# One scan and one readout over both halves of a piece, where its two PSUM banks are neighbours

## The reference

```python
    delta = jax.nn.softplus(jnp.einsum('blr,dr->bld', dt_low, dt_proj_w) + dt_proj_b)
    A = -jnp.exp(A_log)                                   # [512 channels, 16 states]
    dA = jnp.exp(delta[..., None] * A)                    # decay
    dBu = delta[..., None] * B_var[:, :, None, :] * ut[..., None]   # drive
    def step(h, inp):
        da, dbu, c = inp
        h = da * h + dbu                                  # the scan over 512 tokens
        y = jnp.einsum('bdn,bn->bd', h, c)                # the readout
        return (h, y)
    ...
    y = y + ut * D_param
    out_z = y * jax.nn.silu(z)
    return jnp.einsum('bld,ed->ble', out_z, out_proj_w)
```

## Time and profile before

| | us |
|---|---|
| median of 3 runs (lowest, highest) | 2031.44 (2030.55, 2032.27) |
| the profiled execution, its own time | 2028.13 |
| its span, first to last instruction | 2026.3 |
| DVE busy over the span | 1505.6 (74%) |
| PE busy over the span | 1654.3 (82%) |
| ACT, POOL busy over the span | 998.0 (49%), 893.1 (44%) |

### The profile page before, as it was taken

One profiled execution on the slowest core, in us unless ns is written; L12 is line 12 of the kernel. 1 busy time (PEld: TensorE's weight loads), 2 busy tenths in 40 slices (PEclk: granted clock), 3 DMA queues, 4 the chain that ended last, 5 costly groups with the idle time before them and its releaser, 6 DMA issues. The chain is left out here.

```text
span 2026.3 us, 22042 instructions
## 1 busy us (share of the span) xinstructions
PE 1654.3 (82%) x6616; PEld 740.2 (37%) x6616; DVE 1505.6 (74%) x2254; ACT 998.0 (49%) x1524; POOL 893.1 (44%) x662
## 2 busy tenths in 40 slices
PE   7398999999999999999977669596886959678466
PEld 7262534436252543526233124141332414133032
DVE  6436464564546465454658999999999999999998
ACT  3125335252534435252565756657475674747542
POOL 2610000000000000000249887969788796977863
PEclk9998989899898989999888778697887969778677
DMA  5573542526363351627234233424324332441420
GB/s 192 196 118 106 88 137 50 103 88 104 105 103 121 63 133 56 101 99 112 71 114 164 99 121 116 136 77 144 133 99 141 115 118 91 146 135 64 156 94 11
DMA packets 103331, 223.83 MB, mean 110 GB/s; under 512 B 12913, under 2 KB 65266, under 8 KB 99554
## 3 DMA queue, kind: packets, MB, share of 16 engines
q1 hardware_dynamic: 100194, 214.70, 38.4%
q0 software_dynamic: 3072, 8.37, 1.2%
HBM read 169.57 MB, written 53.48 MB: 110 GB/s over the span
## 5 line engine op out<-in xcount | busy, mean ns | idle before, releaser
L1322 POOL TENSOR_TENSOR work<-rep,bc 128x1024 f32<-128x1024 f32 x256 | 597.3, 2355 | 152.3 <-PE ps L1654 135.4
L1551 DVE TENSOR_TENSOR_SCAN ps<-ps,work 128x512 f32<-128x512 f32 x512 | 623.9, 1218 | 19.7 <-ACT ps L1444 11.4
L1444 ACT ACTIVATE ps<-rep,a_neg 128x512 f32<-128x512 f32 x512 | 343.7, 687 | 252.1 <-DVE work L1557 249.4
L830 DVE TENSOR_REDUCE m<-ps 128x1 f32<-128x512 f32 x512 | 327.8, 685 | 161.2 <-PE ps L965 158.3
L717 ACT ACTIVATE prob<-ps 128x1024 f32<-128x1024 f32 x256 | 257.7, 1021 | 235.8 <-PE ps L989 234.1
L1557 DVE TENSOR_TENSOR work<-ps,bc 128x512 f32<-128x512 f32 x512 | 344.1, 672 | 0.0
L1654 PE MATMUL ps<-work,pick 128*32 128x512 f32 x1024 | 181.4, 790 | 168.9 <-DVE work L1557 168.9
L635 POOL TENSOR_TENSOR m_parts<-m,nil 128x16 bf16<-128x16 f32 x32 | 7.1, 221 | 590.0 <-DVE m L830 590.0
L965 PE MATMUL ps<-k_st,q_st 96*128 96x512 bf16 x512 | 201.2, 438 | 31.7 <-DVE m L830 25.7
L1629 PE MATMUL ps<-xn_sb,front_w 128*128 128x512 f32 (+1 forms) x448 | 207.8, 619 | 6.0 <-ACT xn_sb L1378 6.0
L989 PE MATMUL ps<-q_st,k_st 99*128 99x512 bf16 x512 | 169.0, 428 | 0.6
(11 more groups left out here) (203 smaller groups left out, 2006.5 us busy)
## 6 DMA issues: line engine op xcount, KB each, us to landing
rep<-rep_rows SPq DMA_DIRECT2D x128, 512.0 KB, 6.1
front_w<-in_w SPq DMA_DIRECT2D x32, 1024.0 KB, 8.6
bc<-bc_rows SPq DMA_DIRECT2D x32, 512.0 KB, 4.7
rep_rows<-inputs SPq DMA_DIRECT2D x32, 512.0 KB, 5.4
qk_parts<-parts SPq DMA_DIRECT2D x96, 128.0 KB
q_st<-qk_parts SPq DMA_DIRECT2D x96, 128.0 KB, 10.6
k_st<-qk_parts SPq DMA_DIRECT2D x96, 128.0 KB, 11.3
dispatch<-zeros SPq DMA_DIRECT2D x4, 1280.0 KB, 10.5
```

The source lines that it names most:

```text
L830: nc.vector.tensor_reduce(m[:, g % 2, qt, 2 * pair + i:2 * pair + i + 1], ps[:, S0 + i, :], AX.X, ALU.max).then_inc(s_reduced, 1)
L1322: nc.gpsimd.tensor_tensor(work[:, n % WS, :, :], rep[:, g % RS, 2 * h:2 * h + 2, 1, :], bc[:, k, 0, :].unsqueeze(1).broadcast_to([P, 2, SE ...
L1444: nc.scalar.activation(state(m), rep[:, g % RS, 2 * h + i, 0, :], ACT.Exp, scale=a_neg[:, c, 2 * h + i, k:k + 1]).then_inc(decay_ready, 1)
L1551: nc.vector.tensor_tensor_scan(state(m), state(m), work[:, n % WS, i, :], 0.0, ALU.mult, ALU.add).then_inc(state_ready, 1)
```

## The change

`scan_pair` and the new `read` handle a whole piece in one instruction each where its two banks are neighbours (`whole(n)`: the first bank, 2n mod 5, is not the last one). That fails where 2n mod 5 = 4, so for n = 2, 7, 12, ..., 252: 51 of 256 pieces keep separate instructions for the halves, 205 get one scan and one readout of 1024 columns. The order in the loop changes as well: all scanning of piece n, then the other work of that piece, then all reading of piece n.

```diff
+                def pair(n):
+                    first = 2 * n % PLACES
+                    return ps[:, first:first + 2, :]
+
+                def whole(n):
+                    return 2 * n % PLACES + 1 < PLACES
...
+                def scan_pair(n):
+                    dve.wait_ge(decay_ready, 2 * n + 2)
+                    dve.wait_ge(drive_ready, n + 1)
+                    s = pair(n).rearrange("p i t -> p (i t)")
+                    nc.vector.tensor_tensor_scan(s, s, work[:, n % WS, :, :].rearrange("p i t -> p (i t)"), 0.0,
+                                                 ALU.mult, ALU.add).then_inc(state_ready, 2)
+
-                def read(m):
-                    n, i = m // 2, m % 2
+                def read(n):
                     k = n % PER_CHUNK // 2
-                    dve.wait_ge(state_ready, m + 1)
-                    nc.vector.tensor_tensor(work[:, n % WS, i, :], state(m), bc[:, k, 1, :], ALU.mult).then_inc(read_ready, 1)
+                    dve.wait_ge(state_ready, 2 * n + 2)
+                    if whole(n):
+                        nc.vector.tensor_tensor(work[:, n % WS, :, :], pair(n), bc[:, k, 1, :].unsqueeze(1).broadcast_to([P, 2, SEQ]),
+                                                ALU.mult).then_inc(read_ready, 2)
+                    else:
+                        for i in range(2):
+                            nc.vector.tensor_tensor(work[:, n % WS, i, :], state(2 * n + i), bc[:, k, 1, :], ALU.mult).then_inc(read_ready, 1)
...
                 for n in range(BATCH * PIECES):
-                    scan(2 * n)
+                    if whole(n):
+                        scan_pair(n)
+                    else:
+                        scan(2 * n)
+                        scan(2 * n + 1)
                     if n > PER_CHUNK and (n - GATE) % PER_CHUNK == 0:
...
-                    if n:
-                        read(2 * n - 1)
-                    scan(2 * n + 1)
-                    read(2 * n)
-                read(2 * BATCH * PIECES - 1)
+                    read(n)
```

## The result

The changed kernel is slower by a fifth of a per cent: 2034.8 us median of 20 runs (2031.06 to 2039.15), against 2031.38 of 20 runs of the kernel before (2026.59 to 2036.0). The ratio is 1.0021, with a 95% interval of 1.0014 to 1.0028, which is +4.3 us (the two medians lie 3.4 apart). In a second series the ratio was 1.0032 (1.0021 to 1.0043). The forecast was 2029.8, slightly faster; the time is inside the range of 2015 to 2039, but the sign was wrong.

What follows compares the result with a forecast made beforehand. DVE was taken to set the loop's pace, except in six stretches bound by PE. DVE-bound pieces +2.4 us and PE stretches -4 gave -1.6 on the profiled 2028.1; carried to the median, 2029.8 us, range 2015 to 2039.

Steps and rivals of the forecast that it cites:

- g: On DVE, the gap from a scan's end to the readout waiting for it: taken as 0.04 us, ends 0.03 and 0.09.
- whole, plain: Merged pieces with nothing between scan and readout, 106 outside the PE stretches: g - 0.02 us each against 3.43.
- halves, plain: Pieces kept in halves with nothing between scans and readouts, 27 outside the PE stretches: g + 0.10 us more each.
- the rest: The loop without its six PE stretches, where DVE sets the pace: +2.4 us with g = 0.04.
- rival 1: The late readout on DVE costs more, as behind a drain or worse (g 0.09 to 0.13): 2039 us at 0.11; chance 0.20.
- The mergers: On DVE, each merged scan or readout saves a fixed cost of about 0.06 us, 0.12 a piece.
- rival 4: An instruction over two PSUM banks pays for the second, or ACT is late at every softplus: 2046 us; chance 0.05.
- Side work hides the wait: In 32 whole pieces, gate, statistics, maximum or scale between scan and readout hides the wait: -0.11 us each.
- The PE stretch: Third piece to the 17th's scan in six images, PE-bound: 51.9 us each, -4 us in all.
- ACT: At the softplus with its table loads, ACT frees banks 0.2 us before the scan_pair needs them: no cost.
- Rival 2: The readout's wait on DVE costs nothing beyond what every instruction pays: -20 us, 2011.5 us; chance 0.08.
- Rival 3: With PE started sooner, DVE loses its waits in the PE stretch, needing 49.5 us: -14 more, 2015.5 us; chance 0.14.

## Why the prediction was wrong

**The readout's wait, g: the step that failed.** The prediction says: "That last one is the nearest, since it is a release of DVE by a semaphore; I take g = 0.04, and keep 0.03 and 0.09 as ends." In halves that held, with 0.035. In whole pieces g was 0.104, above the upper end. The nearest row was a scan that carries its wait, and was taken for every wait. In the changed code the readout raises its semaphore by 2 and doesn't carry its wait: the run with both semaphores raised by 1 brought g to 0.035 and the loop to +0.7 us, the run with scans merged and readouts in halves had 0.034 behind the same scan. The pieces now count as

```
whole, plain        106 x (3.533 - 3.434)   = +10.5
halves, plain        27 x (3.575 - 3.434)   =  +3.8
whole, side work     32 places, in sum         -2.9
sum                                           +11.4    measured: +11.6
```

Of the 9.2 us between the forecast of the rest and its measured time, g is 106 x (0.104 - 0.04) = 6.8. Another 106 x 0.02 = 2.1 is the paired readout behind such a wait: it holds DVE for 1.141 us from start to start, where 1.12 was forecast from readouts that overlap. So even with g as forecast the sign would hardly have come out: with 0.035 the kernel is still at 1.0010.

The diff showed the raise by 2, and no row of the trace before had such an instruction on DVE's path; the upper end should have had the release and one more instruction of the sequencer. The point from which the sign turns was worked out at g = 0.05, and the forecast stood 0.01 below it. That was thinner ground than a chance of 0.20 for rival 1 says.

**The mergers.** scan_pair 2.289 against 2.29, paired readout 1.22 against 1.20; a scan's merger saves 0.054 (forecast 0.06), a readout's 3.529 - 3.464 = 0.065 (0.06). Right, but for the 0.02 above; and a scan over two PSUM banks costs no more than its slope within one bank gives (1.07 against 1.08), so rival 4 fell. (The 687 ns that the prediction set against 1021 there is not in the earlier trace rows; it is ACT's decay, L1444, which reads SBUF and writes PSUM, the reverse of the other.)

**Side work hides the wait.** Forecast -0.11 in 32 places. From one piece's first scan to the next, in both traces, 29 of the 32 are 0.10 to 0.12 us shorter: the forecast. One is 0.39 shorter, since L1532 takes 0.18 us there in place of 0.47. The two at the loop's start are 0.48 and 0.38 longer, the second with L1532 at 2.29 in place of 1.80. The sum is -2.9 where -3.5 was forecast.

**The PE stretch.** Forecast 51.9 us, measured 52.07 in four of the six (52.11 and 51.40 in the others), the sum -3.8 against -4. The third image shows each step; DVE at its third piece and at its 16th and 17th:

```profile
1322.89 2.29 DVE L1564 TENSOR_TENSOR_SCAN ps<-ps,work 128x1024 f32<-128x1024 f32 x1
1325.08 0.67 DVE L1583 TENSOR_TENSOR sz<-ps,sz 128x512 f32<-128x512 f32 x1
...
1370.40 2.30 DVE L1564 TENSOR_TENSOR_SCAN ps<-ps,work 128x1024 f32<-128x1024 f32 x1 [0.25 <-ACT ps L1444]
1374.95 2.30 DVE L1564 TENSOR_TENSOR_SCAN ps<-ps,work 128x1024 f32<-128x1024 f32 x1 [0.92 <-ACT ps L1444]
```

and PE in front of its seed, with the seed:

```profile
1316.47 9.10 PE L1647 MATMUL ps<-xn_sb,front_w 128*128 128x512 f32 x16
1325.81 1.13 PE L1664 MATMUL ps<-front_w,d_diag 128*128 128x512 f32 x2 [0.23 <-DVE sz L1583]
```

The seed waits for the gate, 1325.81 - 1322.89 = 2.92 behind the scan's start (forecast 2.93; in the earlier trace rows it was 4.34), and the stretch ends 52.06 behind it. The idle time ahead of the seed is 0.23 us, where about 1 was forecast: the 16 matmuls in front of it took 9.10 us where the earlier trace rows has 8.31. The cause is the clock, ahead of the seed and not behind it. First the kernel before (the image of the earlier trace rows), then the changed one, in the columns of the earlier trace rows; the clock is the third figure from the end:

```profile
1433.10:1435.50 2.40, 2.40 (x7) 1.18 (x4) 2.23 (x5) 0.71 (x2) 0.32 (x1) 0.50 0.98 379
1435.50:1441.00 5.50, 5.50 (x14) 2.45 (x13) 5.50 (x8) 1.90 (x3) 5.50 (x3) 1.00 0.79 302
```

```profile
1316.50:1320.50 4.00, 4.00 (x9) 1.82 (x6) 4.00 (x4) 1.66 (x3) 4.00 (x3) 0.50 0.96 352
1320.50:1325.00 4.50, 4.50 (x12) 1.90 (x10) 4.33 (x5) 1.30 (x2) 3.59 (x3) 1.00 0.60 244
```

Both start these matmuls at the lower level of 1.2 GHz (0.50), where they follow each other at 0.85 us, and go to 2.4 GHz on the way, where they follow at 0.43: 2.4 us into them before, 4.0 in the changed kernel. In the six images they take 7.66 to 8.50 us before and 9.08 to 9.20 after. The prediction looked for a lower clock behind the seed only, and put it at nothing; ahead of the seed it cost 0.6 to 1.5 us an image, and was hidden since the seed waits for the gate all the same. That the stretch came out as forecast is luck in this point. From the seed on the clock is at its full level, as the seed's two matmuls of 1.13 us show. At the 17th piece the wait is 0.92, as forecast; at the 16th it is 0.25, a miss. In the image where the 17th piece is in halves the stretch is 51.40: one decay is enough, and the 0.61 of the forecast measure 0.67. The prediction counted both decays in all six. Image by image it took -0.1, -0.6 and four times -0.8; the six measure +0.02, -0.42, -1.30, -0.74, -0.75 and -0.55. That the sum agrees is in part such errors that cancel.

**ACT.** No new wait at the softplus is in the list of waits; it held.

**Rivals.** Rival 1 is what happened: with g = 0.104 its formula gives 133 x 0.104 - 2.9 - 4 = +6.9 us, and the loops have +7.9 and +7.1. Its mechanism was only half seen: it was drawn from a drain, which costs 0.092 behind any scan, while the price of 0.104 here falls on whole pieces alone and the 27 in halves pay 0.035. Rival 2 fell: a wait for the own scan costs 0.035 behind its end, and the next start in front of the end, 0.09, as well. The Trainium skill's page "VectorE: DVE Perf Modes", section "The DRAIN you can't avoid", has it from a test of eight tensor_copy that a semaphore costs nothing extra; here the order alone, which exposes one such wait a piece, makes the piece 0.14 us longer, and the measurement decides. The prediction also held the starts ahead of the recorded end against that section. There it read too little of it: the same section says that a next operation that is not held starts earlier, and the trace agrees, by 0.09 us. Rival 3 fell in the changed kernel. In the version with only the last readout first it came about in part: there DVE loses its waits at the gate and at the 16th piece in four of the six images and keeps 1.0 us at the 17th, and these stretches come to 50.33 us, where it put 49.5.

What stays open: why a readout holds DVE for 0.01 to 0.02 us more where the one wait is exposed; why the run with the semaphores raised by 1 gave back 4.5 us in time where its pieces give 7.7; and how much of the scatter of about 4 us between runs is L1532's luck.

## What to carry to other kernels

A consumer directly behind its producer on one engine loses the overlap of the two and pays for the wait, here 0.14 us of 3.4; a merger that saves 0.05 to 0.12 is not worth that order. With one other instruction between them it is, where that engine sets the pace: 3.38 us against 3.43. Look at how a wait is encoded: one that rides on its instruction costs less than one that stands alone, and the count by which an instruction raises its semaphore can decide which it is. Merge where the engine itself sets the pace, and keep halves where another engine hands over half the data at a time.

## What the runs showed of the hardware

- In these traces a DVE instruction that raises a semaphore by 1 carries one wait; all that raise by 2 have the wait as an instruction of its own in front. Behind an own scan this starts the next one 0.104 us after the end, against 0.035 carried and 0.092 with a drain. Where the wait is long fulfilled, it costs nothing measured (0.9991, 0.9980 to 1.0002).
- A tensor_tensor_scan over 1024 columns in two PSUM banks takes 2.289 us, one over 512 takes 1.218: 1.07 for the second half, where the slope within one bank (16 and 512 columns) gives 1.08, so nothing is seen for the bank.
- A tiny tensor_scalar (128x32, 0.18 us) on DVE takes up to 2.3 us when it meets a POOL product in progress, and ends 0.04 us behind it; the reciprocal behind it keeps its 0.35, also in the two images of seven where POOL's next product is already in progress. The Trainium skill's page "SBUF — State Buffer", section "Who interferes with whom", says that such a tensor_scalar and a GpSimd instruction exclude each other for a whole instruction, whoever comes first. The trace agrees: 1.07 us until POOL's product ended. With it on ACT (0.22 us in each image) and two drains fewer, the time fell from a ratio of 0.9961 to 0.9918.
- TensorE's 16 matmuls (128x512) that follow an idle time of 3.2 to 4.2 us and one short sum start at the lower granted clock (0.50), 0.85 us apart, and go on at full clock, 0.43 apart. How far into them the clock rose changed with no edit of TensorE's list: the group took 7.66 to 8.50 us in the kernel before and 9.08 to 9.20 in the changed one.
